# Half of the alignment masks built by ScalarE, and two orders changed, in the second stage of a decoder layer

## The reference

```python
x = _layernorm(x + _L0_attn_ref(x, ...), axis=-1)            # stage 1
x = _layernorm(x + _L0_xattn_ref(ctx_1024, x), axis=-1)      # stage 2
x = _layernorm(x + _L0_ffn_ref(x, ...), axis=-1)             # stage 3
...
    def _align_one(small, large):          # per batch: small 77x256, large 256x256
        D = _pairwise_euclidean(small, large)
        R = _dtw_cost(D)
        i_idx, j_idx, valid = _backtrack(R, T_small, T_large)
        contrib = small[i_idx] * valid[:, None].astype(small.dtype)
        expanded = jnp.zeros((T_large, d), dtype=small.dtype).at[j_idx].add(contrib)
...
        mean = x.mean(axis=0)              # stage 3 begins with a norm over all 32 batches
        var = x.var(axis=0)
```

## Time and profile before

| | |
|---|---|
| median of 3 runs | 2917.5 us (2917.36 to 2917.92) |
| the profiled execution, and its span | 2916.79 us, 2915.0 us |
| first mask begun, last norm begun | 389.1 us, 480.68 us |
| busy share of the whole span: PE, DVE, POOL, ACT | 91%, 76%, 30%, 25% |

### The profile page before, as it was taken

One profiled execution on the slowest core, in us unless ns is written; L12 is line 12 of the kernel. 1 busy time (PEld: TensorE's weight loads), 2 busy tenths in 40 slices (PEclk: granted clock), 3 DMA queues, 4 the chain that ended last, 5 costly groups with the idle time before them and its releaser, 6 DMA issues.

```text
span 2915.0 us, 104470 instructions
## 1 busy us (share of the span) xinstructions
PE 2654.6 (91%) x43108; PEld 2296.2 (79%) x43108; DVE 2219.8 (76%) x7508; ACT 734.3 (25%) x1274; POOL 877.4 (30%) x700
## 2 busy tenths in 40 slices
PE   6961168799999999999999999999999999999996
PEld 5851146688888888888888888888888888888895
DVE  5668966877777777777777777777777888877754
ACT  4740024322222222222222222222222222222210
POOL 1330065233333233323332333233333333333332
PEclk9985579999999999999999999999999999999997
DMA  5550337400000000000000000000000000000000
GB/s 175 174 164 16 57 113 183 71 13 13 13 11 10 13 13 10 13 14 13 14 13 14 13 14 13 14 13 14 13 14 13 14 13 13 14 13 13 10 10 12
DMA packets 84639, 99.52 MB, mean 34 GB/s; under 512 B 6189, under 2 KB 74702, under 8 KB 84046
## 3 DMA queue, kind: packets, MB, share of 16 engines
q1 hardware_dynamic: 84190, 92.94, 11.4%
HBM read 65.13 MB, written 27.79 MB: 32 GB/s over the span
## 4 chain that ended last, share of the span: by engine, by line
PE 81%; issue 1%; DVE 1%; ACT 0%; POOL 0%; DVEq 0%; ACTq 0%; POOLq 0%
PE bank L1037 32%; PE bank L1071 31%; PE bank L1055 9%; PE bank L1008 8%; PE bank L1023 1%; PE bank L995 1%; DVE hot L1254 0%; DVE shared L1266 0%; POOL hot L974 0%; ACT L1156 0%; ACT gelh L1156 0%; ACT x2T L1137 0%; DVEq L1275 0%; ACT xnT L1129 0%; DVEq L1286 0%
## 5 line engine op out<-in xcount | busy, mean ns | idle before, releaser
L974 POOL TENSOR_TENSOR hot<-hot,valsT 128x512 f32<-128x512 f32 x512 | 732.8, 1450 | 1663.8 <-DVE hot L1254 1663.8
L1037 PE MATMUL bank<-x2T,shared 128*64 128x128 f32 x16384 | 952.3, 274 | 1.6 <-ACT gelh L1156 1.4
L1037 PEld LDWEIGHTS bank<-x2T,shared 128*64 128x64 f32 x16384 | 890.6, 137 | 23.6 <-issue 8.7
L1254 DVE TENSOR_TENSOR hot<-places,valsT 128x1024 f32<-128x1024 f32 x512 | 654.3, 1319 | 0.2 <-issue 0.2
L1071 PE MATMUL bank<-up,shared 64*128 64x256 f32 x4096 | 448.9, 378 | 1.5 <-DVE shared L1266 1.5
L1071 PE MATMUL bank<-up,gelh 64*128 64x256 f32 x4096 | 446.4, 377 | 0.0
L1071 PEld LDWEIGHTS bank<-up,shared 64*128 64x128 f32 x4096 | 396.6, 188 | 58.9 <-issue 11.4
L1071 PEld LDWEIGHTS bank<-up,gelh 64*128 64x128 f32 x4096 | 395.2, 187 | 56.2 <-issue 11.5
L1055 PE MATMUL bank<-hot 64*64 64x64 f32 x16384 | 303.9, 224 | 33.3 <-POOL hot L974 17.0
L1055 PEld LDWEIGHTS bank<-hot 64*64 64x64 f32 x16384 | 268.7, 137 | 82.0 <-issue 82.0
L1266 DVE TENSOR_TENSOR shared<-bank,shared 128x512 f32<-128x512 f32 x256 | 164.9, 686 | 176.4 <-PE bank L1055 176.0
(11 more groups left out here) (147 smaller groups left out, 2163.3 us busy)
## 6 DMA issues: line engine op xcount, KB each, us to landing
x_scratch<-x_sb SPq DMA_DIRECT2D x64, 256.0 KB, 2.1
xT_sb<-in_xT SPq DMA_DIRECT2D x32, 256.0 KB, 2.8
x_sb<-in_x SPq DMA_DIRECT2D x32, 256.0 KB, 2.8
x_again<-x_scratch SPq DMA_DIRECT2D x32, 256.0 KB, 2.7
x_tile<-x_scratch SPq DMA_DIRECT2D x32, 256.0 KB, 3.7
up<-in_table SPq DMA_DIRECT2D x2, 4096.0 KB, 36.5
yo<-x_scratch SPq DMA_DIRECT2D x32, 256.0 KB, 2.8
out_y<-yo SPq DMA_DIRECT2D x32, 256.0 KB, 2.1
```

Source lines behind the costliest of these rows:

```text
L974: pool.tensor_tensor(lo, lo, valsT[:, par, 2, TQ * q:TQ * (q + 1), None].to_broadcast([P, TQ, NK]), ALU.mult).then_inc(gated_ready, 1)
L1037: mm = pe.matmul(ps_h[q % 2][half(c), i, :], dnT[:, k, lo // 2, half(lo % 2)], x2T[:, par, k, c, :], start=(k == 0), stop=(k == CC - 1))
L1254: dve.tensor_tensor(hot[:, q % SLOTS], places[:, None, None, :].to_broadcast([P, 2, TQ, NK]), valsT[:, par, 0:2, TQ * q:TQ * (q + 1), None ...
```

## The change

The lower side of the mask moves from POOL to ACT. ACT keeps four times the lower bound, and computes with two Relus `above = relu(1 - relu(4*lo - 4*j))`, which is one where j >= lo. POOL computes the upper side and multiplies the two. POOL's wait for `warp` moves behind its comparison, and a drain is added behind the product. ACT's list has now four parts, with the root ahead of the norm; DVE's list has the aggregation ahead of the channel statistics. SP and PE keep their orders.

```diff
--- before.py
+++ after.py
@@ -125,6 +125,8 @@
         bounds_ready = sem("bounds_ready")
 
         x1_in = [sem(f"x1_in{i}") for i in range(2)]
+        short_ready = sem("short_ready")
+        above_ready = sem("above_ready")
         mask_ready = sem("mask_ready")
         warp_mm = sem("warp_mm")
         shift2_ready = sem("shift2_ready")
@@ -573,6 +575,8 @@
             wq_rows = sw("wq_rows", [P, NPH, C])
             keysT = sw("keysT", [P, NPH, NK])
             below = sw("below", [S2, 2, T])
+            short_of = sw("short_of", [S2, 2, T])
+            above = sw("above", [S2, 2, T])
             mask = sw("mask", [S2, 2, T])
             x1_sb = sw("x1_again", [P, 2, NT, C])
             st2 = sw("st2", [P, 2, NT, 6])
@@ -648,12 +652,13 @@
 
                 def masks(b, par):
 
-                    if later(b, 2):
-                        pool.wait_ge(warp_mm, b - 1)
-                    pool.tensor_scalar(mask[:, par, :], iota[0:S2, :], bounds[0:S2, 0, b:b + 1], None, ALU.is_ge)
                     pool.tensor_scalar(below[:, par, :], iota[0:S2, :], bounds[0:S2, 1, b:b + 1], None, ALU.is_le)
                     pool.drain()
-                    pool.tensor_tensor(mask[:, par, :], mask[:, par, :], below[:, par, :], ALU.mult).then_inc(mask_ready, 1)
+                    pool.wait_ge(above_ready, b + 1)
+                    if later(b, 2):
+                        pool.wait_ge(warp_mm, b - 1)
+                    pool.tensor_tensor(mask[:, par, :], above[:, par, :], below[:, par, :], ALU.mult).then_inc(mask_ready, 1)
+                    pool.drain()
                 for b in range(NB):
                     masks(b, b % 2)
 
@@ -667,7 +672,26 @@
                     act.wait_ge(dnT_mm, q + 1)
                     act.activation(dnT[:, :, 2 * q:2 * q + 2, :], ps_dn[q % 2], ACT.Copy).then_inc(dnT_ready, 1)
                 act.wait_ge(bounds_mm, 1)
-                act.activation(bounds[:, :, :], ps_bounds[:, :, :], ACT.Copy).then_inc(bounds_ready, 1)
+                act.activation(bounds[:, 0, :], ps_bounds[:, 0, :], ACT.Copy, scale=4.0)
+                act.activation(bounds[:, 1, :], ps_bounds[:, 1, :], ACT.Copy).then_inc(bounds_ready, 1)
+                act.wait_ge(bounds_ready, 1)
+
+                def ramps(b, par):
+
+                    if later(b, 2):
+                        act.wait_ge(above_ready, b - 1)
+                        rest(act, act_rests)
+                    act.activation(short_of[:, par, :], iota[0:S2, :], ACT.Relu, scale=-4.0,
+                                   bias=bounds[0:S2, 0, bass.ds(b, 1)]).then_inc(short_ready, 1)
+
+                def aboves(b, par):
+
+                    act.wait_ge(short_ready, b + 1)
+                    if later(b, 2):
+                        act.wait_ge(mask_ready, b - 1)
+                    rest(act, act_rests)
+                    act.activation(above[:, par, :], short_of[:, par, :], ACT.Relu, scale=-1.0, bias=ones[0:S2, 0:1])\
+                        .then_inc(above_ready, 1)
 
                 def std(b, par):
                     act.wait_ge(var2_ready, b + 1)
@@ -685,7 +709,7 @@
                                               scale=rs2[:, par, t:t + 1], bias=nb2[:, par, t:t + 1])
                     last.then_inc(x2_ready, 1)
 
-                pipeline(act, [(norm, 4, 4), (std, 3)], 8, unroll=4)
+                pipeline(act, [(ramps, 0), (std, 3), (aboves, 0), (norm, 4, 4)], 8, unroll=4)
                 act.wait_ge(bnvar_ready, 1)
                 act.activation(bn_tmp[:, :], bn_mv[:, :, 1], ACT.Sqrt, bias=eps_col[:, :]).then_inc(bnstd_ready, 1)
 
@@ -837,7 +861,7 @@
                                             in_=ps_x2T[par][:, c, :])
                     last.then_inc(bn_done, 1)
 
-                pipeline(dve, [(recip, 3), (stats, 2, 4), (shift, 3), (chan_stats, 5), (aggr, 2)], 8, unroll=4)
+                pipeline(dve, [(recip, 3), (stats, 2, 4), (shift, 3), (aggr, 2), (chan_stats, 5)], 8, unroll=4)
                 dve.drain()
                 for c in range(CC):
                     last = dve.bn_aggr(out=bn_mv[:, c, :], in_=bn[:, c, :, :].rearrange("p b s -> p (b s)"))
```

More of the change, by code:

```diff
@@ L649, in masks @@
                 def masks(b, par):
+                    pool.tensor_scalar(below[:, par, :], iota[0:S2, :], bounds[0:S2, 1, b:b + 1], None, ALU.is_le)
+                    pool.drain()
+                    pool.wait_ge(above_ready, b + 1)
                     if later(b, 2):
                         pool.wait_ge(warp_mm, b - 1)
-                    pool.tensor_scalar(mask[:, par, :], iota[0:S2, :], bounds[0:S2, 0, b:b + 1], None, ALU.is_ge)
-                    pool.tensor_scalar(below[:, par, :], iota[0:S2, :], bounds[0:S2, 1, b:b + 1], None, ALU.is_le)
+                    pool.tensor_tensor(mask[:, par, :], above[:, par, :], below[:, par, :], ALU.mult).then_inc(mask_ready, 1)
                     pool.drain()
-                    pool.tensor_tensor(mask[:, par, :], mask[:, par, :], below[:, par, :], ALU.mult).then_inc(mask_ready, 1)
                 for b in range(NB):
```

## The result

The changed kernel takes 2925.0 us (median of 12 runs), the kernel before 2918.0 us in the runs beside it: ratio 1.0026, 95% interval 1.0018 to 1.0034. It is slower by about 7 us, where 2922 and +4.5 us were forecast.

A forecast was written before the change was run, and what follows sets the result against it. POOL was taken to bound the batch pipeline at 2.68 us a batch; afterwards a ring at 2.86: +4.3 over 24 batches, +0.5 start, -0.3 end, sum +4.5 on 2916.8, plus 0.7 for the median: 2922 us, range 2914 to 2927.

The forecast's parts named there:

- a ring through all engines: Kernel before: norm, store, load, warp, statistics, norm three batches later; 7.93 us, 2.64 a batch, against POOL's 2.68.
- rival 1: Batch pipeline: only the two-batch chain through turn holds, loads land early; pace 2.70, +0.7 us, 2918; chance 20%.
- PE's floor: PE in the batch pipeline: 2.40 us from one turn to the next without idle time, the most POOL's relief allows.
- rival 2: Batch pipeline: POOL's relief pays in full, PE sets the pace at 2.40; -6.7 and -0.7 us, 2910; chance 10%.
- the piece from statistics to norm: From a batch's statistics to the next norm: aggregation 0.91, root 0.28, second Relu 0.18, norm 0.35; 1.72 us for 0.86.
- My row: Trace row used for the Relu's length on ACT: Identity of 16x256 with bias from a tile, 0.47 us; 0.46 taken.
- The long ring: Norm, store, load, warp, statistics, norm three batches later, in the changed kernel: 8.58 us, 2.86 a batch, setting the pace.
- the short ring: Norm, turn, warp, statistics, norm two batches later, in the changed kernel: 5.39 us, 2.70 a batch.
- The sum: Total: 24 x 2.86 - 64.4 = +4.3 us, with first and last batches +4.5 us, giving 2922 us.
- the start: Batch pipeline up to the fourth norm: first norm about +0.1 us, fourth norm +0.5 us.
- the end: Last four batches, without Relus ahead of their norms: 9.1 us in place of 9.4, -0.3 us.
- Rival 3: Batch pipeline: loads take 3.3 us, 3.01 a batch, 2926; or PE's clock falls to 1.2 GHz, above 2934; chance 20%.

The follow-up runs named there:

- Loads ahead alone: Kernel before, with four buffers for the reloaded x1 and the store five steps behind the load instead of three: 2915.0 us, 0.9977 to 0.9995 of before.
- the norm first: Changed kernel with ACT's list as norm, root, first Relu, second Relu: 2917.3 us, 0.9997 to 1.0016 of before.
- orders alone: Kernel before with root ahead of norm and aggregation ahead of channel statistics, masks left to POOL: 2920.3 us, 1.0002 to 1.0025 of before.
- Relus alone: Changed kernel with norm at the head of ACT's list and DVE's list as before: 2917.2 us, 0.9993 to 1.0011 of before.
- aggregation last: Changed kernel with DVE's list as before, aggregation behind the channel statistics: 2927.8 us, 1.0023 to 1.0050 of before.

## Why the prediction was right, and where it was off

- **POOL bounds the kernel before, and a ring through all engines is close behind.** Right. Loads ahead alone left the pace at 2.69, and with POOL relieved and the norm first it stood at 2.67: two limits at nearly one place. I had the ring at 2.64; with the norm first it is 8.07 us, 2.69. For rival 1 I wrote that few of PE's waits name the DMA. That was misread: 12 of its 23 waits from 389 to 480 us do, 7 name the mask, and 4 no releaser:

```profile
PE bank L724 <- POOL mask L656: 5.2, 7, 3.1
PE bank L724 <- DMA x_again<-x_scratch: 4.8, 12, 0.7
```

- **POOL's relief by itself gains nothing.** Right as to the change; its size was misjudged. I read PE's floor as 2.40 us from one pair of turns. It is 2.29, and with it the relief is worth 11.8 us in the pipeline once both rings are short. In rival 2 I had 7.4 us for that.
- **The orders lengthen the piece from statistics to norm from 0.86 to 1.72.** Right: 1.80 measured over 20 batches (before, 0.96 over as many; my 0.86 was one case). Of the 0.08 more, 0.05 is from Relu to norm (0.40 for 0.35) and 0.02 from root to Relu (0.20 for 0.18); the Relu takes 0.50 us instead of my 0.46. For its length the Trainium skill (ScalarE: Activation LUTs, What ACT_TABLE_LOAD costs) was nearer: its 280 ns and 0.833 ns a column give an estimate of 0.49 for 256 columns, and the trace agrees with 0.495 and 0.500. My row was of 16 partitions out of PSUM. Its section Table sets: the hidden batching unit, by which Relu is in every set, fits as well: no table load stands among the Relus and roots.
- **The long ring sets the pace, 2.86.** Right in mechanism: 1.16 + 0.80 + 2.94 + 2.02 + 1.80 = 8.72 us over 20 batches, 2.91 each, with the warp close behind its load each time, and the pace falls to 2.68 once this ring is opened. Against my 8.58 the terms that grew are the load (2.94 for 2.84, of one case) and the piece with the Relu. Over 24 batches this is 1.3 us. The next limit, the short ring, was not far: opened alone, the long one gives back 0.23 us a batch.
- **The sum, +4.5.** 24 x (2.913 - 2.682) = +5.5; the start +0.5, as forecast (the fourth norm is 18.66 us behind the bounds, before 18.16); the end -0.5 for my -0.3. Sum +5.5. The medians differ by 7.0. Of the remaining 1.5 us a part is in what follows the last norm (+1.1 in the profiled pair) and isn't of the pipeline; late landings are a candidate for the rest.
- **Rival 3, the clock.** I gave it 20%, together with slower loads, for all batches, and against waits of 0.5 us the trace was right. What I left out is the rare long wait. In five of the 14 profiled executions one reload took 3.5 to 4.5 us to land (405 to 470 us, median 2.7 to 2.8). In two of the five the loads ran ahead, and PE did not wait for it. In the three others, all of kernels with the root ahead of the norm, it waited 1.44, 1.47 and 2.26 us; behind the last two its clock fell to 0.50 and the event cost 3 to 4 us, behind the first the clock stayed at 1.00 and it cost about 1.3. The Trainium skill (TensorE: Matmul & The Clock Gate, HAM oscillation — how this bites in real kernels) describes such a loop, a wait for a DMA and then slow products, with waits of 3 to 5 us. The row with 2.26 us of waiting and a clock of 0.50 agrees with its course, but here shorter waits did it. Why 1.47 us sufficed and 1.44 did not is open. Whether the kernel before has such events less often, since POOL's pace leaves it slack, these few executions can't tell.

That the loss was in the orders and not in the masks' move was in the prediction only as terms of a sum. The runs separate it: orders alone +3.1 us in the pipeline, Relus alone -0.3, both +5.5, since the second Relu costs only once the root stands ahead of the norm.

## What to carry to other kernels

An engine that is full hides the ring behind it. Before relieving it, add up one turn of each dependency ring from the timeline, divide by the batches it spans, and compare that with the engine's pace; relief is worth only the distance to the next of these. Count work and transfer times, not waits: from event to event a turn always adds up to the pace. In a list of parts for an engine with time to spare, what counts is what stands between the arrival of an input and the instruction that feeds other engines: put that instruction first and everything else behind it. And a store that is issued ahead of an unrelated load on one queue ties the load to the store's producer. Loads issued well ahead also take the rare late one out of the path.

## What the runs showed of the hardware

- ACTIVATE of 77x256 from SBUF with the bias from a tile: 0.50 us, and the next one starts 0.40 us after it.
- A reload of 256 KB took 2.94 us from its issue to the first product that used it, on average of 20 (2.82 to 3.09). It landed after 2.7 to 2.8 us in the median, and once each in five of 14 executions only after 3.5 to 4.5 us.
- After waits of 1.47 and of 2.26 us, PE's next products ran at 1.2 GHz. After one of 1.44 us (aggregation last) they did not, and idle times of up to 0.8 us in each batch of the changed kernel left the clock at 1.00.
